# Four stacked graph layers: the mask's -1/0 adjacency and the last residual made by accumulating transfers, eight couples masked by VectorE, queues reordered

## What is computed

```python
x = _layernorm(x + _L0_gnn_ref(x, adj, ...))   # one head, leaky relu, softmax over the neighbours
x = _layernorm(x + _L1_gnn_ref(x, adj, adj, ...))   # eight heads
x = _layernorm(x + _L2_gnn_ref(x, adj, ...))   # mean over the neighbours, its own affine norm and relu
x = _layernorm(x + _L3_gnn_ref(x, adj, ...))
# layer 3, 4 heads of 32:
Wh = jnp.einsum('bsf,hfd->bhsd', features, W)
scores = jnp.einsum('bhsd,bhtd->bhst', Wh, Wh) / jnp.sqrt(jnp.float32(D))
scores = jnp.where(adj_matrix[:, None, :, :] > 0, scores, NEG_INF)
attn = jax.nn.softmax(scores, axis=-1)
h = jnp.einsum('bhst,bhtd->bhsd', attn, Wh)
```

## Time and profile before

| | us |
|---|---|
| median of 3 runs | 2534.38 |
| lowest, highest | 2531.88, 2535.02 |
| the profiled execution's own time | 2537.21 |
| its span in the trace | 2535.5 |
| mean granted clock of TensorE | 0.965 |

### The profile page before, as it was taken

One profiled execution on the slowest core, in us unless ns is written; L12 is line 12 of the kernel. 1 busy time (PEld: TensorE's weight loads), 2 busy tenths in 40 slices (PEclk: granted clock), 3 DMA queues, 4 the chain that ended last, 5 costly groups with the idle time before them and its releaser, 6 DMA issues.

```text
span 2535.5 us, 56744 instructions
## 1 busy us (share of the span) xinstructions
PE 2281.9 (90%) x23694; PEld 1528.0 (60%) x23813; DVE 2173.3 (86%) x4125; ACT 1944.8 (77%) x2161; POOL 167.5 (7%) x104
## 2 busy tenths in 40 slices
PE   3668999989999999999989899998989999998966
PEld 3557556575765658575665757656485765657341
DVE  3688799898988989898898989889898989989756
ACT  2758798787879878787987778788787878878714
POOL 0000001001000100100010010001001000100000
PEclk9788999999999999999999999999999999999978
DMA  6504133222323322232332123233222323101000
GB/s 129 134 18 118 42 85 77 62 74 43 102 68 85 83 65 64 43 101 68 85 84 66 62 43 101 68 85 76 60 77 42 102 68 85 45 33 52 9 17 9
DMA packets 192976, 172.80 MB, mean 68 GB/s; under 512 B 137168, under 2 KB 171088, under 8 KB 191696
## 3 DMA queue, kind: packets, MB, share of 16 engines
q1 hardware_dynamic: 191424, 135.61, 19.5%
q0 software_dynamic: 1296, 33.56, 6.5%
HBM read 151.78 MB, written 42.53 MB: 77 GB/s over the span
## 4 chain that ended last, share of the span: by engine, by line
PE 64%; DVE 14%; issue 9%; ACT 8%; DMA 3%; POOL 2%; SPq 1%; POOLq 0%; ACTq 0%; DVEq 0%
PE kp L821 15%; PE kp L804 10%; PE fp L707 9%; PE fp L646 9%; PE kp L797 6%; PE kp L752 3%; DVE weight L1317 3%; ACT ramp L994 3%; DMA shared<-shared 2%; DVE bstat L1127 2%; ACT weight L1037 2%; PE kp L749 2%; POOL bsmall L541 2%; PE fp L600 2%; PE fp L593 1%
## 5 line engine op out<-in xcount | busy, mean ns | idle before, releaser
L994 ACT ACTIVATE ramp<-s1row,tbig 128x1024 bf16<-128x1024 f32 x864 | 921.0, 1143 | 85.6 <-DVE weight L1317 85.5
L1037 ACT ACTIVATE weight<-kp,shift 128x1024 f32<-128x1024 f32 x512 | 543.9, 1114 | 196.2 <-PE kp L804 194.7
L1317 DVE TENSOR_TENSOR weight<-ramp,AT 128x2048 bf16<-128x2048 bf16 x512 | 609.6, 1221 | 75.9 <-ACT ramp L994 52.1
L821 PE MATMUL kp<-weight,w 128*33 128x512 f32 x2048 | 490.9, 600 | 9.5 <-ACT weight L1037 5.7
L707 PEld LDWEIGHTS fp<-vh_parts,weight 128*128 128x128 bf16 x8192 | 402.8, 100 | 130.5 <-DVE weight L1317 66.7
L707 PE MATMUL fp<-vh_parts,weight 128*128 128x102 bf16 x8192 | 431.9, 212 | 40.0 <-DVE vh L1325 24.7
L804 PE MATMUL kp<-shared 32*128 32x512 f32 x2048 | 298.0, 652 | 9.8 <-ACT weight L1037 7.5
L821 PEld LDWEIGHTS kp<-weight,w 128*33 128x33 f32 x2048 | 97.7, 110 | 321.4 <-issue 255.9
L646 PEld LDWEIGHTS fp<-features,weight 128*128 128x128 f32 x2048 | 234.9, 194 | 40.9 <-issue 40.3
L646 PE MATMUL fp<-features,weight 128*128 128x129 f32 x2048 | 240.7, 279 | 16.9 <-DVE weight L1228 16.9
L1456 DVE SCALAR_TENSOR_TENSOR weight<-AT,weight 128x1024 f32<-128x1024 bf16 x182 | 214.6, 1222 | 36.7 <-ACT weight L1037 36.7
(11 more groups left out here) (179 smaller groups left out, 2527.3 us busy)
## 6 DMA issues: line engine op xcount, KB each, us to landing
s1row<-s_rows_dram SPq DMA_DIRECT2D x128, 512.0 KB, 4.1
adj_bf_dram<-in_adj_dram POOLq DMA_DIRECT2D x15, 2048.0 KB, 13.7
x<-in_x_dram SPq DMA_DIRECT2D x16, 512.0 KB, 7.5
xfT<-s_row_dram SPq DMA_DIRECT2D x16, 512.0 KB, 3.6
shared<-shared SPq DMA_DIRECT2D x32, 256.0 KB, 3.5
out_dram<-elu SPq DMA_DIRECT2D x16, 512.0 KB, 4.5
adj_bf_dram<-in_adj_dram POOLq DMA_DIRECT2D x2, 1024.0 KB, 10.8
s_rows_dram<-weight SPq DMA_DIRECT2D x16, 32.0 KB
```

Of the source, the lines that this page charges most:

```text
L821: last = pe.matmul(kp[side(h), 0, :], w3[:, (2 * J + x) * H3 + h, :], weight3[:, w % P_RING, x * HALF:(x + 1) * HALF], start=(J == 0 and x ...
L994: act.activation(ramp[:, u % R_RING, :], s1row[:, h % S_RING, :], ACT.Relu, bias=tbig1[:, jt, h:h + 1], scale=BIG).then_inc(ramp_ready.sem, 1)
L1037: act.activation(weight3[:, w % P_RING, :], kp[:, 1 + 2 * (w % 2):3 + 2 * (w % 2), :].rearrange("p a n -> p (a n)"), ACT.Exp, bias=shift3[ ...
L1317: dve.tensor_tensor(edges[:, u % B_RING:u % B_RING + 2, :], ramp[:, u % R_RING:u % R_RING + 2, :], AT[:, third, jt:jt + 2, :], ALU.min).th ...
```

## The change

The subtraction of 1 leaves VectorE: GpSimd's queue issues a transfer that adds a tile of -1 (`minus`, 128 x 256 bf16, read again and again) onto the third of `AT`, 128 x 32 runs of 256 elements (512 bytes). It waits for the same signal (layer 2's sum made). The residual leaves VectorE too: a transfer adds x3 onto `x4`, for all batches but the last; layer 2's norm then waits for it before it overwrites that half of x3. Three more couples (4, 6 and 8) are masked by VectorE. All tables are new, and the last two of the 19 sections have a table of their own. The core of the diff (`of` gives a signal's count for a batch; the tables of TensorE, ScalarE and VectorE are left out, and pieces of the order stand below):

```diff
-    MASKED = (10, 11, 12, 13, 14)
+    MASKED = (4, 6, 8, 10, 11, 12, 13, 14)
...
+        minus = sb("minus", [P, 2 * P], BF16)
...
-        STAGE = (0, 0, 0, 0, 0, 0, 0, 0, 0, 0, 0, 0, 0, 0, 0, 0, 0, 0, 0)
+        STAGE = (0, 0, 0, 0, 0, 0, 0, 0, 0, 0, 0, 0, 0, 0, 0, 0, 0, 1, 1)
...
         ON_POOL = [
-            (dict(adjacency=3, rstd0=4, rstd1=5, rstd2=0, rstd3=1, rstd_tail=2),),
+            (dict(adjacency=7, mask3=3, residual3=2, rstd0=5, rstd1=6, rstd2=0, rstd3=1, rstd_tail=4),),
+            (dict(adjacency=-1, mask3=0, residual3=3, rstd0=-1, rstd1=-1, rstd2=1, rstd3=2, rstd_tail=4),),
         ]
         ON_SP = [
-            (dict(adjacency=1, far=6, out=10, sources=[2, 3, 4, 5, 7], sources_ahead=[12, 13, 14], spread_row=9,
-                 store_row=8, store_sources=11, x=0),),
+            (dict(adjacency=0, far=7, out=10, sources=[2, 3, 4, 5, 6], sources_ahead=[12, 13, 14], spread_row=9,
+                 store_row=8, store_sources=11, x=1),),
...
+            pool.memset(minus[:], -1.0).then_inc(consts_made, 1)
...
+            def layer3_mask(b, third):
+                if b == 0:
+                    pool.wait_ge(consts_made, 4)
+                pool.wait_ge(sum2_made.sem, sum2_made.of(b))
+                pool.dma_start(AT[:, third].rearrange("p t (c n) -> p (t c) n", n=2 * P),
+                               minus[:].unsqueeze(1).broadcast_to([P, T * T // 2, 2 * P]), accum_op=ALU.add) \
+                    .then_inc(mask3_made.sem, 16)
+
+            def layer3_residual(b):
+                pool.wait_ge(o3_ready.sem, o3_ready.of(b))
+                pool.dma_start(x4[:], x3[:, b % 2], accum_op=ALU.add).then_inc(residual3_added.sem, 16)
...
             def layer2_norm(b):
                 dve.wait_ge(brstd_ready.sem, brstd_ready.of(b, 2))
+                if b >= 2:
+                    dve.wait_ge(residual3_added.sem, residual3_added.of(b - 2))
...
-            def layer3_mask(b, third):
-
-                dve.wait_ge(sum2_made.sem, sum2_made.of(b))
-                dve.tensor_scalar(AT[:, third], AT[:, third], -1.0, None, ALU.add).then_inc(mask3_made.sem, 1)
-
...
+                    if w == 2 * masks(b)[0]:
+                        dve.wait_ge(mask3_made.sem, mask3_made.of(b))
...
-            def layer3_residual(b):
-                dve.wait_ge(o3_ready.sem, o3_ready.of(b))
-                dve.tensor_tensor(x4[:], x4[:], x3[:, b % 2], ALU.add).then_inc(back_last.sem, 1)
-                dve.wait_ge(back_last.sem, back_last.step())
+            def layer3_stats(b):
+                if b < NB - 1:
+                    dve.wait_ge(residual3_added.sem, residual3_added.of(b))
+                else:
+                    dve.wait_ge(o3_ready.sem, o3_ready.of(b))
+                    dve.tensor_tensor(x4[:], x4[:], x3[:, b % 2], ALU.add).then_inc(dve_last_added, 1)
+                    dve.wait_ge(dve_last_added, 1)
                 layer_stats(back_last, x4, tstat, tsmall, tvar_ready)
```

More of the change, by code:

```diff
@@ L354, in graph_stack @@
         exp3_ready = signal("exp3_ready", U3)
-        mask3_made = signal("mask3_made", 1)
+        mask3_made = signal("mask3_made", 16)
         masked3_ready = signal("masked3_ready", 2 * len(MASKED))
@@ L361, in graph_stack @@
         o3_ready = signal("o3_ready", 1)
+        residual3_added = signal("residual3_added", 16)
         y2_first = signal("y2_first", 1)
@@ L372, in graph_stack @@
         dve_back = sem("dve_back")
+        dve_last_added = sem("dve_last_added")
         block = ctx.enter_context(nc.Block())
@@ new lines, in graph_stack @@
+            (dict(cut1=[-1, -1], cut1_second=[-1, -1], elu=-1, exp3=[4, 5, 6, 7, 8, 9, 10, 11, 12, 13, 15, 16, 17, 18,
+                 19, 20, 21, 22, 24, 25, 26, 27, 28, 29, 30, 31, 33, 34, 35, 36, 37, 38], exps0=-1, exps1=-1,
+                 first2=-1, out3=[14, 23, 32, 39], prepare0=-1, project0=[-1, -1, -1], project1=-1, project3=2,
+                 ramps=[-1, -1, -1, -1, -1, -1, -1, -1, -1, -1, -1, -1, -1, -1, -1, -1, -1, -1, -1, -1, -1, -1, -1,
+                 -1, -1, -1, -1, -1, -1, -1], ramps_ahead=[-1, -1], second2=-1, self2=0, sources1=-1, sum1=[-1, -1,
+                 -1], turn0=[-1, -1], turn1=-1, turn2=-1, turn3=1, unit0=[-1, -1, -1, -1, -1, -1, -1, -1], wide3=3),),
@@ new lines, in graph_stack @@
+            (dict(affine2=2, columns1=[-1, -1], cut1=[-1, -1], cut1_third=[-1, -1], divide1=-1, elu1=-1, finish0=-1,
+                 finish1=-1, finish3=4, head1=[-1, -1, -1, -1, -1, -1, -1, -1], lengths3=6, low2=-1, masked3=[10, 11,
+                 13, 14, 15, 16, 17, 18, 19, 20, 21, 22, 23, 24, 25, 26], maxima1=-1, maxima3=7, maximum0=-1,
+                 most0=-1, norm0=-1, norm1=-1, norm3=5, out2=0, prepare=-1, ramps=[-1, -1, -1, -1, -1], relu2=3,
+                 rest2=-1, shift0=-1, shift3=9, shifts1=-1, stats2=1, stats3=8, tail3=12, top0=-1, top1=-1, unit0=[-1,
+                 -1, -1, -1, -1, -1, -1, -1], unit1=[-1, -1, -1, -1, -1, -1, -1, -1, -1, -1, -1, -1, -1, -1, -1, -1,
+                 -1, -1, -1, -1, -1, -1, -1, -1, -1, -1, -1, -1, -1, -1, -1, -1], z0=-1),),
@@ L422, in graph_stack @@
+            (dict(adjacency=-1, far=0, out=1, sources=[-1, -1, -1, -1, -1], sources_ahead=[-1, -1, -1], spread_row=-1,
+                 store_row=-1, store_sources=-1, x=-1),),
         ]
@@ L575, in step @@
                     load_adjacency(n + 1)
+                if k is not None and s == at["mask3"]:
+                    layer3_mask(k, (r + 2) % 3)
+                if m is not None and m < NB - 1 and s == at["residual3"]:
+                    layer3_residual(m)
                 if f is not None and s == at["rstd1"]:
@@ L1517, in step @@
                     layer3_finish(m, k)
-                if m is not None and s == at["residual3"]:
-                    layer3_residual(m)
-                if k is not None and s == at["mask3"]:
-                    layer3_mask(k, (r + 2) % 3)
+                if m is not None and s == at["stats3"]:
+                    layer3_stats(m)
                 for v in range(PAIR_UNITS):
```

47 lines of the change are left out of this document (27 added, 20 removed).

## The result

The changed kernel takes **2647.51 us** (median of 4 runs, 2646.3 to 2648.22), the kernel before 2533.13 beside it: ratio 1.0451, 95% interval 1.0433 to 1.0469. That is 114 us slower, outside the range of the prediction, and 7.5 us beyond the far end of its rival of the late mask (2640).

A forecast was written before the change was run, and what follows sets the result against it. TensorE was taken to set the period of 147.26 us a batch, with room on VectorE. 2537.2 - 38 + 9 + 14 = 2522, less 2.8 for the runs' median: forecast 2519 us, range 2497 to 2625.

The forecast's parts named there:

- rival of the late mask: Mask lands 5.3 to 9.0 us late at layer 3's first scores: +50 to +106, 2585 to 2640 us; chance 0.28.
- The bound of the kernel before: TensorE's length sets the period where layer 3's scores are made: it idles 0.3 us of 60, VectorE 8.4.
- The couples: -38 and +9, together -29: Three couples' mask matmuls leave TensorE, 2.55 us a batch, -38; waiting for VectorE's masking, 0.19 a couple, gives back +9.
- The mask's operation and the residual off VectorE: Per batch VectorE loses 2.30 and 1.22 us and gains six masking ops of 1.22: +3.8, still less than TensorE.
- The mask by DMA: Mask issued on GpSimd's queue behind both layer 2 roots at about 1138, wanted at 1153.42: an allowance of 15.4 us.
- I take 13.7 behind 1.8 of residual: Mask's landing time, taken from the adjacency's load: lands at 1153.5, just where the far copy lets TensorE go.
- the 17.1 taken as the upper bound: Adding transfer's landing if reading the target doubles the busy time: 14.4 + 2.7 us, behind a residual of 3.6.
- The far copies: +14: Far heads' copy ahead of the first scores, 3.5 us, 5.4 at most, slowed beside the mask: 0.9 a batch, +14.
- GpSimd's issue: 0.56 us, rival 28.7: Transfer's issue on GpSimd takes 0.56 us; rival: 28.7 for 4096 runs, landing 16 late, +211, 2746 us, chance 0.07.
- Adjacency's load and SyncE's order: hidden: Load moved behind layer 1's rstd, landing 1231.5 before its 1238.69 transpose; SyncE's x lands by 1255.1, before its turn.
- VectorE as the bound: 2553: Rival: VectorE's 3.8 us more a batch all shows, 57 - 38 = +19, 2553 us; chance 0.05.
- the signs named: Right: 480 line-840 weight loads, AT<-minus landing in 12 to 15 us; wrong: TensorE waiting 3 us, issue of several us.

The follow-up runs named there:

- experiment 3: The changed kernel with the mask made by a VectorE operation ahead of layer 3's lengths instead of the transfer: 2545.67 us, ratio 1.0047.
- experiment 7: The changed kernel with the mask's transfer issued ahead of both layer 2 roots and only five masked couples, as before the change: 2540.2 us, ratio 1.0022.
- Experiment 8: The kernel before, own orders and five couples, with only the mask made by an adding transfer issued ahead of layer 2's roots: 2535.81 us, ratio 0.9999.
- experiment 6: The changed kernel with the mask's transfer ahead of layer 2's roots and the residual added by VectorE again: 2512.93 us, ratio 0.9914.
- the mask first: The changed kernel with GpSimd issuing the mask's transfer ahead of both layer 2 roots, the residual's behind them: 2512.93 us, ratio 0.9921.
- experiment 2: The changed kernel with the mask's transfer, in the same place and pieces, a plain copy of zeros without addition: 2556.85 us in one run.
- experiment 5: The changed kernel with the mask's transfer ahead of layer 2's roots and the adjacency's load right behind the tail's root: 2519.04 us, ratio 0.9934.
- nine couples: The changed kernel with the mask's transfer ahead of layer 2's roots and couple 9 masked by VectorE as well: 2523.48 us, ratio 0.9958.
- experiment 10: The changed kernel with a longer mask source, so 2048 pieces of 1 KB instead of 4096 of 512 B: 2620.44 us, ratio 1.0333.

## Why the prediction was wrong, step by step

**The bound of the kernel before** (TensorE sets the period, VectorE has room) held for the stretch of the scores: the couples' term rests on it and came out right. Ahead of the first scores VectorE has no room in the new orders (experiment 3).

**The couples: -38 and +9, together -29.** Measured 27 (experiment 7). The hand-over was put at 0.19 us a couple; what shows is the net, 9.1 us a couple over 15 batches against the 9.7 of the sum. Right, once the mask is in time.

**The mask's operation and the residual off VectorE.** The prediction named only their busy time. Experiment 8 shows that the operation had been free in the old orders, and experiment 6 that the residual is free in the new ones. The prediction gave neither a gain and was right there, without a reason for the middle of the run; and experiment 3 shows a price of 33 us in the new orders that no step of the prediction names.

**The mask by DMA: this step failed.** Its issue was put at 23.4 us behind layer 2's first operation (1138 - 1114.6); it came at 1180.88 - 1157.88 = 23.0. The place of the want, 38.8 behind that operation, was read rightly from the kernel before (37.6 at the median with the mask first). What failed is the term "I take 13.7 behind 1.8 of residual". The choice fell on the adjacency's load as the nearest row, since it too reads twice what it writes. But it has some 80 packets where the mask has 4096 pieces, and it adds to nothing. Measured: a copy in these pieces takes 12.4 us, near the load's 13.7; the addition makes it 22.6, and 19.7 with no residual ahead of it, above the 17.1 taken as the upper bound. That bound doubled a copy put at 7.2 us of busy time; the copy of experiment 2 leaves 12.4 - 2.7 = 9.7, and twice that plus 2.7 is 22.1, an estimate that nearly meets the 22.6. The residual ahead and the far copies beside are some 2.9 us of it (22.6 - 19.7), where the prediction's upper side had 3.6 and 2.1, and 1.6 for a source row. The text's own bound "with the source row and the far copies in between, 1162.4, 9.0 late" gave +106, 2640 us; the result is 7.5 above that, though the mask landed 6.6 us late (1203.32 - 1157.88 = 45.4 against 38.8) and not 9.0. At the median the first scores come 46.0 us behind layer 2's first operation and before 38.8, 7.2 later: 15 x 7.2 - 29 = +79. The clock behind the wait, which no term names, adds 15 x 1.5 = 22 (last section), and the new orders the 6 of experiment 7. That is 107 of the 113 above the forecast's base of 2534.4; the rest stays open. So the rival's mechanism, its place and nearly its size were on the table, and the weights were wrong: a row that lacks the one new feature of the operation, the read of the target, was taken as its nearest.

**The far copies: +14.** They take 8.6 us at the median, above "5.4 at most", but in the changed kernel that lies under the wait for the mask. Where the late transfer is short enough to land in time, in experiment 2, they take 5.2, and TensorE's wait for them is 47.2 us where it was 28.5: 19 us, near the 14. With the mask first they take 4.1 and the wait is 27.4, so the term is nothing.

**GpSimd's issue: 0.56 us, rival 28.7.** The second step that failed. Measured 3.44 for the mask and 0.93 for the residual. The rival in proportion was eight times too high, the forecast six times too low; and what it costs was in neither: it holds up VectorE (last section). Experiment 2 shows that this matters for the forecast: with a landing of 12.4 us, below the 13.7 taken, the kernel takes 2556.85 us and not 2519. So the landing was the term that made most of the 114 us, but a right one would not have made the forecast right. Of the 38 us, the far copies are 5 more than was summed and the stretched normalisation 15 x 1.2 = 18; the kernel of experiment 7, in which neither occurs, is 6 slower than the kernel before; the rest stays open.

**Adjacency's load and SyncE's order: hidden.** Right for the load (experiment 5); no run moves SyncE's order by itself.

**VectorE as the bound: 2553.** Not what happened in the changed kernel, but it is near: with nine couples the time turns upward.

Of the signs named, 480 weight loads of line 840 came as said, and the wait of TensorE on AT<-minus of over 3 us and the issue of several us were those that were to show it wrong.

## What to carry to other kernels

Work moved to a transfer was free here only when it was issued as soon as its input was ready. Here the input was complete 23 us before the issue, and one place in a queue's order was the difference between 21 us gained and 114 lost. So price an adding transfer from the read of its target, not from the nearest copy; where no row has it, put the likeliest time near the upper bound, and ask first whether the order can make its length not matter. And an operation that leaves an engine gains only if the engine does not then wait in its place: look at what the next operation on it needs.

## What had not been expected

**The issue stretches a normalisation.** VectorE beside the mask's issue, which runs from 1180.88 to 1184.32 in the changed kernel:

```profile
1180.94 4.27 DVE L1187 TENSOR_SCALAR x<-yb,bsmall 128x128 f32<-128x128 f32 x8
```

Elsewhere these eight operations take 2.14 us. Single ones are held up, not all of them a little (min, median, max in ns; the second row is the same operation at layer 2's first normalisation, with no such issue beside it):

```profile
L1187 DVE TENSOR_SCALAR x<-yb,bsmall x128: 327/344/1771, 247.3 to 2552.6; 128x128 f32<-128x128 f32 x128
L1187 DVE TENSOR_SCALAR yb<-yb,bsmall x128: 334/339/346, 233.9 to 2542.3; 128x128 f32<-128x128 f32 x128
```

Their group over the whole run, in the changed kernel and with the mask first:

```profile
L1187 DVE TENSOR_SCALAR x<-yb,bsmall 128x128 f32<-128x128 f32 x128 | 66.3, 885 | 1.6 <-POOL bsmall L568 1.5
```

```profile
L1187 DVE TENSOR_SCALAR x<-yb,bsmall 128x128 f32<-128x128 f32 x128 | 34.2, 344 | 1.6 <-POOL bsmall L568 1.5
```

32 us in all, 2.1 a batch, for an issue of 3.4; 1.1 a batch for one of 2.45 (experiment 10: 50.3 us) and 1.2 for one of 1.89 (experiment 2: 51.7). With the mask first, the same issue (1104.71 to 1107.90) runs beside the first two of these, which take what they take elsewhere:

```profile
1105.24 2.16 DVE L1436 SCALAR_TENSOR_TENSOR yb<-kp,deg,yb 128x128 f32<-128x128 f32 x8
1107.43 2.36 DVE L1360 TENSOR_TENSOR weight<-ramp,AT 128x2048 bf16<-128x2048 bf16 x2
1114.23 2.14 DVE L1187 TENSOR_SCALAR yb<-yb,bsmall 128x128 f32<-128x128 f32 x8
```

The last of these rows lies beside the mask's transfer, which lands near 1124.4, and behind its issue: it is the issue that stretches the operation, not the transfer. The prediction looked for VectorE holding up GpSimd; it was the other way round. The Trainium skill, "SBUF — State Buffer", section "SBUF: two separate sides", has both directions: the port pair that the two engines share is an exclusive lock, held by whichever starts first; on VectorE's side it concerns an operation in a two-port mode, and one with two SBUF inputs only against a GpSimd operation that reads SBUF. The runs agree in which operations are stretched: the float32 tensor_scalar is, the bf16 tensor_tensor with two inputs in SBUF and the scalar_tensor_tensor that reads PSUM are not. No row tells in which mode an operation runs, and the longest one takes 1.77 us beside an issue of 3.4, so VectorE got through once before the issue's end. In the changed kernel the stretch lies under the wait for the mask; in experiment 2 it is paid.

**The clock falls behind the wait.** Busy times by stretch, at the first scores of the changed kernel:

```profile
1203.77:1205.00 1.23, 1.23 (x3) 0.30 (x2) 0.00 (x0) 0.00 (x0) 0.00 (x0) 0.50 0.90 333
1205.00:1207.20 2.20, 2.20 (x11) 0.61 (x11) 0.00 (x0) 0.00 (x0) 0.00 (x0) 0.55 0.05 19
1207.20:1213.00 5.80, 5.75 (x67) 3.10 (x68) 3.78 (x4) 5.71 (x6) 0.00 (x0) 1.00 0.01 1
```

TensorE idled 8 us here. Then the granted clock is 0.50 to 0.55, its lower level of 1.2 GHz, for about the first 3.2 us of work. The mask matmuls and the scores of that couple take 1.49 + 1.93 = 3.4 us, where they took 0.81 + 1.07 at a clock of 1.00 in the batch of the earlier trace rows. With the mask first TensorE idles 1.92 us at this place, and the clock falls too, a little later:

```profile
1142.36:1145.06 2.70, 2.70 (x12) 0.60 (x12) 2.70 (x3) 1.33 (x3) 0.00 (x0) 0.74 0.63 194
1145.06:1148.00 2.94, 2.94 (x49) 2.94 (x46) 2.21 (x4) 2.79 (x3) 0.00 (x0) 0.66 0.01 3
```

So the fall is not new, only more frequent and often longer. By the clock's records it comes at the first scores of all 15 batches in the changed kernel, of 11 with the mask first and of 6 in the kernel before. There it lasts 3.1 to 5.9 us of work in the changed kernel, and at most 3.4 in the other two. From the first couple's first matmul to the second couple's it takes 6.3 us in the mean of the 15 batches, 5.35 with the mask first and 4.85 before. Those 1.5 us a batch more than before stand where the three couples save their 1.8 (27 us over 15), so the stretch of the scores looked unchanged. Against the kernel with the mask first, the first scores come 46.0 us behind layer 2's first operation and not 37.6 (medians), 8.4 later, and the clock adds 1.0: together the (2309.1 - 2170.1) / 15 = 9.3 us a batch that the late issue costs, more than the 7.8 that the wait for the mask shows.
